# Attention scores from two float32r parts instead of three bf16 parts, the two heads of a pair on the two halves of the TensorE array

## What is computed

```python
q = proj(x1t, Wq, bq); k = proj(x2t, Wk, bk); v = proj(x2t, Wv, bv)
scores = jnp.einsum('bhqd,bhkd->bhqk', q, k) / jnp.sqrt(D_HEAD)   # 512 x 512 a head
attn = jax.nn.softmax(scores, axis=-1)
out = jnp.einsum('bhqk,bhkd->bhqd', attn, v)
...
x = x + jnp.tanh(g_xattn[0]) * xattn(_layernorm(x), ctx_2048, ...)
x = x + jnp.tanh(g_ffn[0]) * ffn(_layernorm(x), ...)               # 8 experts, top 2, one shared
```

## Time and profile before

| | |
|---|---|
| median of 3 runs | 1526.43 us (1523.7 to 1527.67) |
| span of the profiled execution | 1525.5 us; the profile gives no other time of it |
| attention, turns with both kinds of score matmul (i = 0 to 30) | about 47 to 886 us |
| last turn of attention | to about 925 us |
| experts | to the end |

### The profile page before, as it was taken

How to read it: one execution, slowest core, us unless ns; L and a number is a source line. 1 busy time by engine, 2 the same in 40 slices (tenths; PEclk the granted TensorE clock), 3 DMA queues, 4 the chain that set the end, 5 groups by cost and what they waited for, 6 DMA issues and landing times.

```text
span 1525.5 us, 23419 instructions
## 1 busy us (share of the span) xinstructions
PE 1475.7 (97%) x7362; PEld 669.8 (44%) x7362; DVE 887.8 (58%) x1802; ACT 782.5 (51%) x1531; POOL 814.5 (53%) x1241
## 2 busy tenths in 40 slices
PE   5999999999999999999999999989999999999997
PEld 1233333333333333333333328767755454545443
DVE  5888888888888888888888842512221121211111
ACT  2577777777777777777777771100022222222221
POOL 6346675766757667576674443375134444444442
PEclk9999999999999999999999999999999999999999
DMA  6566667766676666765666424785345455554554
GB/s 153 128 160 168 175 167 183 180 161 162 162 177 163 168 163 162 178 170 152 165 154 167 117 92 162 248 213 121 113 76 97 85 96 88 93 91 88 92 90 61
DMA packets 159304, 215.10 MB, mean 141 GB/s; under 512 B 28162, under 2 KB 102416, under 8 KB 158160
## 3 DMA queue, kind: packets, MB, share of 16 engines
q1 hardware_dynamic: 137136, 175.78, 44.9%
q0 software_dynamic: 17952, 37.30, 14.0%
q10 hardware_dynamic: 4096, 0.53, 0.2%
HBM read 126.12 MB, written 86.91 MB: 140 GB/s over the span
## 4 chain that ended last, share of the span: by engine, by line
PE 87%; DMA 6%; DVE 2%; issue 1%; POOL 1%; ACT 1%; SPq 1%; ACTq 0%; POOLq 0%; DVEq 0%
PE bank L1140 16%; PE bank L1062 16%; PE bank L1033 14%; PE bank L1011 14%; PE bank L1160 10%; PE bank L1135 5%; PE bank L996 4%; PE bank L1038 3%; DMA arena<-ht_d 2%; PE bank L1049 2%; PE bank L1000 2%; DMA pv_d<-arena 1%; PE bank L1148 1%; DVE row_max L696 1%; PE bank L1020 1%
## 5 line engine op out<-in xcount | busy, mean ns | idle before, releaser
L696 DVE TENSOR_REDUCE row_max<-bank 128x1 f32<-128x512 f32 x1024 | 664.9, 682 | 111.6 <-PE bank L1011 102.5
L892 ACT ACTIVATE arena<-bank 128x512 f32<-128x512 f32 x1024 | 564.5, 612 | 205.5 <-PE bank L1033 194.0
L1011 PE MATMUL bank<-arena 96*128 96x512 bf16 x1024 | 392.2, 384 | 7.8 <-DVE row_max L696 5.5
L1033 PE MATMUL bank<-arena 98*128 98x512 bf16 x1024 | 387.2, 380 | 2.9 <-ACT arena L892 1.8
L1062 PE MATMUL bank<-arena 128*32 128x512 f32 x2048 | 272.7, 605 | 1.0 <-ACT arena L892 0.7
L1140 PE MATMUL bank<-arena 128*128 x568 | 255.5, 592 | 0.0
L834 DVE TENSOR_TENSOR arena<-arena,bank 128x256 f32<-128x256 f32 x103 | 43.4, 421 | 331.7 <-ACT arena L943 327.9
L943 ACT ACTIVATE arena<-bank 128x256 f32<-128x256 f32 x103 | 39.6, 384 | 378.2 <-PE bank L1140 224.9
L604 POOL DMA_INDIRECT out<-xs,ids x71 | 112.3, 1581 | 226.3 <-ACT xs L954 184.0
L1160 PE MATMUL bank<-arena 128*128 (+1 forms) x412 | 193.8, 593 | 0.9 <-ACT arena L959 0.9
L523 POOL TENSOR_TENSOR arena<-arena 128x512 bf16<-128x512 f32 x62 | 71.6, 1155 | 226.7 <-ACT arena L884 224.0
(11 more groups left out here) (122 smaller groups left out, 1252.4 us busy)
## 6 DMA issues: line engine op xcount, KB each, us to landing
arena<-parts_q SPq DMA_DIRECT2D x64, 256.0 KB, 4.8
pv_d<-arena SPq DMA_DIRECT2D x32, 512.0 KB, 6.3
parts_k<-arena SPq DMA_DIRECT2D x96, 128.0 KB
arena<-parts_k SPq DMA_DIRECT2D x32, 384.0 KB, 4.9
parts_q<-arena SPq DMA_DIRECT2D x96, 128.0 KB
arena<-in_w SPq DMA_DIRECT2D x8, 1536.0 KB, 8.9
h_d<-arena SPq DMA_DIRECT2D x33, 256.0 KB, 6.7
out<-xs SPq DMA_DIRECT2D x33, 256.0 KB, 2.5
```

The lines of the kernel that those rows point to most:

```text
L696: nc.vector.reduce_max(row_max[b % 2][:, u:u + 1], m_ps[(STEPS * b + u) % M_BANKS][:], AX_X).then_inc(s_mx, 1)
L892: nc.scalar.activation(probs[group % 3][:, j, :], e_ps[n % E_BANKS][:], ACT.Exp, scale=float(DH) ** -0.5).then_inc(s_exp, 1)
L1011: nc.tensor.matmul(m_ps[n % M_BANKS][:], q_stack[b % 3][0:STACK, h, qt * P:(qt + 1) * P], k_stack[b % 3][0:STACK, h, :], start=True, stop= ...
L1033: nc.tensor.matmul(e_ps[n % E_BANKS][:], k_stack[b % 3][0:SHIFTED, h, kt * P:(kt + 1) * P], q_stack[b % 3][0:SHIFTED, h, :], start=True, s ...
```

## The change

Keys and queries are now split into two float32r parts, HI and LO. The stacks are `K_PARTS` HI, LO, HI and `Q_PARTS` HI, HI, LO: three times 16 = 48 rows, 50 with the maximum's two. Two heads form a pair: the even head lies on partitions 0 to 49, the odd one on 64 to 113, so a head's matmul reads only rows of one half of the array. In the free dimension there are four pairs instead of eight heads. ACT no longer casts; POOL makes HI (one tensor_scalar) and LO (one subtraction). The order on TensorE changes: both kinds are issued in twos, the two heads of a pair right behind each other, at even steps. For the maxima the order of tiles is now pair, query tile, head, and the column of `row_max` is chosen so that the transposed maxima come out by head. `row` starts four DMAs instead of two.

```diff
-HI, MID, LO = range(3)
-K_PARTS = (HI, MID, LO, HI, MID, HI)
-Q_PARTS = (HI, HI, HI, MID, MID, LO)
+HI, LO = range(2)
+K_PARTS = (HI, LO, HI)
+Q_PARTS = (HI, HI, LO)
...
+PAIR = 2
+READS = PAIR * (len(runs(K_PARTS)) + len(runs(Q_PARTS)))
 STACK = len(K_PARTS) * DH
+SIDE = P // PAIR
 SHIFTED = STACK + 2
...
             def split(b, n):
+                pool.wait_ge(s_evac, 3 * b + n + 1)
+                pool.wait_ge(s_wr[n], 2 * DMA * b)
+                hi, lo = parts[n]
+                nc.gpsimd.tensor_scalar(hi[:], proj[n], 1.0, 0.0, ALU.mult, ALU.add).then_inc(s_hi, 1)
                 pool.wait_ge(s_hi, 2 * b + n + 1)
...
+                nc.gpsimd.tensor_tensor(lo[:], proj[n], hi[:].bitcast(F32), ALU.subtract).then_inc(s_lo, 1)
...
                 act_e.wait_ge(s_mr, 2 * b + half + 1)
-                for n in range(2):
-                    act_e.dma_start(q_stack[b % 3][STACK + n:STACK + n + 1, half * GROUP:(half + 1) * GROUP, :],
-                                    m_rows[half][:, n, :]).then_inc(s_row[half], DMA)
+                for e in range(PAIR):
+                    for n in range(2):
+                        row = e * SIDE + STACK + n
+                        act_e.dma_start(q_stack[b % 3][row:row + 1, 2 * half:2 * half + 2, :].bitcast(F32),
+                                        m_rows[half][e * 2 * KT:(e + 1) * 2 * KT, n, :].bitcast(F32)
+                                        ).then_inc(s_row[half], DMA)
...
             def max_scores(b, u):
-                h, qt = divmod(u, KT)
+                p, qt, e = u // (PAIR * KT), u // PAIR % KT, u % PAIR
+                rows = slice(e * SIDE, e * SIDE + STACK)
...
-                nc.tensor.matmul(m_ps[n % M_BANKS][:], q_stack[b % 3][0:STACK, h, qt * P:(qt + 1) * P],
-                                 k_stack[b % 3][0:STACK, h, :], start=True, stop=True).then_inc(s_ms, 1)
+                nc.tensor.matmul(m_ps[n % M_BANKS][:], q_stack[b % 3][rows, p, qt * P:(qt + 1) * P],
+                                 k_stack[b % 3][rows, p, :], start=True, stop=True).then_inc(s_ms, 1)
...
                 for s in range(STEPS):
-                    if is_b(i):
+                    if s % PAIR == 0 and is_b(i):
                         exp_scores(i, s)
-                    if is_b(i + 1):
+                        exp_scores(i, s + 1)
+                    if s % PAIR == 0 and is_b(i + 1):
                         max_scores(i + 1, s)
+                        max_scores(i + 1, s + 1)
```

More of the change, by code:

```diff
@@ L9 @@
 BF16 = mybir.dt.bfloat16
+F32R = mybir.dt.float32r
 ALU = mybir.AluOpType
@@ L104, in build @@
         xs = sb("xs", [P, B, L])
+        with ExitStack() as stacks:
+            q_stack, k_stack = ([stacks.enter_context(nc.sbuf_tensor(f"{n}_stack{i}", [P, HEADS // PAIR, L], F32R))
+                                 for i in range(3)] for n in "qk")
+            parts = [[stacks.enter_context(nc.sbuf_tensor(f"{n}_{part}", [P, L], F32R)) for part in ("hi", "lo")]
+                     for n in "kq"]
         arena = sb("arena", [P, ARENA])
-        a = Arena(arena)
-        q_stack = [a.take(HEADS * L // 2, BF16).rearrange("p (h l) -> p h l", h=HEADS) for _ in range(3)]
-        k_stack = [a.take(HEADS * L // 2, BF16).rearrange("p (h l) -> p h l", h=HEADS) for _ in range(3)]
+        a = Arena(arena, 6 * HEADS // PAIR * L + 4 * L)
         probs = [a.take(GROUP * L).rearrange("p (j l) -> p j l", j=GROUP) for _ in range(3)]
@@ L113, in build @@
         proj = [a.take(L) for _ in range(2)]
-        rest = a.take(L)
-        parts = [[a.take(L // 2, BF16) for _ in range(3)] for _ in range(2)]
         wq, wk, wv = (a.take(P) for _ in range(3))
@@ L220, in build @@
         s_ones = sem("s_ones")
+        s_stack = sem("s_stack")
         s_x = [sem(f"s_xin{i}") for i in range(4)]
@@ L430, in _ @@
                 if is_b(i + 3):
-                    for part in (HI, MID, LO):
+                    for part in (HI, LO):
                         write(i + 3, 0, part)
@@ L701, in maxima_rows @@
                 if b:
-                    dve.wait_ge(s_row[half], 2 * DMA * b)
+                    dve.wait_ge(s_row[half], 2 * PAIR * DMA * b)
                 return chain(
```

80 lines of the change are left out of this document (29 added, 51 removed).

## The result

| | before | after |
|---|---|---|
| median of 4 runs | 1525.07 us (1520.54 to 1527.67) | 1751.8 us (1730.12 to 1769.05) |
| ratio | | 1.139, interval 1.1327 to 1.1454 |
| span of the profiled execution | 1525.5 us | 1757.5 us |

The ratio compares before with the two faster executions of after (1730.12 and 1744.38 us, mean granted clock 0.925 and 0.903); the other two, 1759.21 and 1769.05 us at 0.890 and 0.885, lie over 1.5% above the fastest, and the first of them is the profiled one. By this ratio the change costs 212 us, by the two medians 227, and not 19: the time is outside the range either way. The four runs lie 39 us apart, against 7 before: the change also made the kernel's time scatter.

A forecast was written before the change was run, and what follows sets the result against it. TensorE bounds the kernel before; after, its loop through three banks: 8 x 2.77 + 4.4, plus 0.6, 0.4 and 0.1, makes 27.7 us a turn against 27.1. Over 31 turns +19 us, start -1.3: 1544 us, range 1505 to 1590.

The forecast's parts named there:

- rival (3): TensorE's granted clock falls for half the time, about +150 us: 1680 us; chance 0.07.
- The chain that takes over: TensorE's loop through three banks of each kind bounds a group of four steps: 2.77 us without the other products.
- E3: Fourth exponentials' product of a four-step group; waits until ACT has read the first one's bank.
- M3: Fourth maxima product of a four-step group; waits for DVE's reduction of the first one's bank, starts at 1.46 us.
- X: TensorE's other products (projections, token transposes, logits, transposed maxima): 4.4 us a turn, added in full after the change.
- p: Weight load that can't be hidden because its instruction waits: 0.09 us more, bounds 0 and 0.19.
- ACT's queue: DMA starts on it hold it 0.56 us each and delay exponentials: 0.4 us a turn, bounds 0 and 2.3.
- The evacuations' 0.6: ACT's copies of K and Q, with the tokens' copy, delay the exponentials behind them: 0.6 us a turn.
- The start: Preparing batch 0's Q parts takes two operations in place of four and ends 1.3 us earlier.
- rival 2: The halves don't overlap or a product takes two passes: turn 29.1 us, 1587 us; chance 0.16.
- rival 4: The loop isn't the bound, TensorE runs ahead and DVE's 23.2 us a turn are: 1405 us; chance 0.04.
- Rival (1): Products run concurrently but waits are shorter, weight loads and DMA starts hidden: 1488 to 1506 us; chance 0.18.

The follow-up runs named there:

- e12: Kernel before, each score product reading 48 of its 96 or 98 rows, order and columns unchanged: 1787.87 us against 1525.62.
- e2: Kernel after plus two overwritten products on half of the rows ahead of the exponentials' products of steps 2, 6, 10 and so on: 1721.99 us, ratio 1.0812.
- e3: Kernel after plus two overwritten 128-row products ahead of the exponentials' products of steps 2, 6, 10 and so on: 1700.93 us, ratio 1.0714.
- e4: Kernel after with two DMA starts in `row` instead of four, each for both halves of the array: 1685.97 us, ratio 1.0591.
- e5: Kernel after with projections, transposed maxima, token transposes and logits moved to other steps, away from the values groups: 1645.02 us, ratio 1.0825.
- e9: Same as e8, but the maxima's rows start at steps 22 and 7 instead of 24 and 9: 1563.48 us, ratio 1.0268.
- e8: Kernel after with two DMA starts in `row` and the values groups moved to the middle of the four steps: 1595.3 us, ratio 1.049.
- e10: Same as e9 plus one 128-row fill product in each of eight places: 1587.11 us, ratio 1.0409; one of four executions took 2131.07.
- e11: Same as e9 plus two 128-row fill products in each of eight places: 1645.01 us, ratio 1.079.

## Why the prediction was wrong

**The step that failed first is the clock.** The sum has no term for it: it took the granted clock as 1.00 in all turns ("PEclk 1.0 in the turns"), and rival (3) had 0.07. The clock was 0.84 on average from 100 to 1100 us, and the fall cost some 108 us; rival (3)'s price of about +150 was of the right order. The argument against it was that streams would fill 63% of a group, "nearer the last turn" than to the place where DVE set the pace. It compared time under streams and never asked how many rows those streams use: e12, with the streams of before on half of the rows, loses at least 229 us. In after two products on half of the rows run side by side, so the rows in use at a time are about as before, but for half of the time, and waits fill the rest; e2 and e3 show that both count, and how much each does isn't known. And the last turn, my example of a safe clock, runs at 0.50 after the change (1110 to 1150 us). I should have seen that no row of before has long stretches of products on half of the rows, so that rows 1 and 9 bear on neither side.

**The second step that failed is the turn at full clock, 27.7 us against 30.2. The chain that takes over: right, 1.4 us a turn too short.** TensorE left being the bound, and E3 and M3 wait for the readers of E0 and M0, as walked. E3 came 1.18 us behind E0, forecast 1.16 (M3's 1.38 less the 0.22 between them). But the group without X is 2.94 us, not 2.77. The term is p: it was charged at M3 alone, but E0 is also a product whose load isn't hidden. Its record lasts 0.50 us where E2's lasts 0.39, M0 starts 0.34 behind it and not 0.22, and ACT starts 0.53 behind it and not 0.42. In all M3 starts 1.53 behind E0 (601.29 to 602.82), forecast 1.46, and the values 0.41 behind M3, whose load isn't hidden either, forecast 0.31. 8 x 0.17 = 1.4 us. That E3 came out almost as forecast is in part luck: the walk had ACT start 0.11 too early and p ahead of E3's start, where it shows in E3's record instead. What the prediction cites for p (the Trainium skill, TensorE: Matmul & The Clock Gate, weight-path perf modes) speaks of FP32 and doesn't name float32r; the records of 0.18 to 0.19 us are what settles it.

**X: a cost that wasn't in the sum.** Each X product stands 0.1 us longer ahead of a score product: a projection 1.06 (592.64 to 593.70) against 0.96, the logits 0.99 against 0.92, the transposed maxima 0.2 against 0.11, and V 1.09 against 0.89. The seven of them make 0.8 us. e12 has it without float32r.

**ACT's queue: too small.** The starts of the DMAs stand 0.66 us apart (four from 594.24 to 596.90), not 0.56, and the extra ones cost 1.2 us a turn (e4), where I took 0.4 for them and 0.1 for late landings. The bound of 2.3 covered it. The chosen value assumed that the group at step 9 gives the delay back; e4 changed both places at once and doesn't tell them apart. The evacuations' 0.6 wasn't isolated; e5 moved all of X, its turns at full clock are 27.8 to 29.9 us, and how much of that is the evacuations' is open. Sum: 27.7 + 1.4 + 0.8 leaves 0.3 for the queue's part beyond what I took, against 30.2 measured; the terms overlap, so e4's 1.2 can't be added on top of all the others.

**The start: wrong sign.** DVE's copy to float32r took 2.03 us at 15.28 (the same copy for K took 0.43 at 7.67; here POOL was clearing `k_stack` from 15.23 on, which may be why), so LO was ready at 18.04, where before the third subtraction ended at 18.47; the first maxima's product came at 29.15 (28.41 before), behind a wait of 3.33 us for the parts of Q read back from DRAM (2.07 before), and the first exponentials' at 55.46 behind a 1.09 us wait for the rows of the maxima (51.26 before): 4.2 us later, not 1.3 earlier.

**What was right.** One pass for a float32r product, two halves side by side (rival 2 is out: one product in 0.39, two in 0.40); DVE isn't the bound (rival 4 is out: busy 23.62 of 30 us in a turn at full clock, 79% where 84% was forecast). Rival (1), shorter waits, is out too, as p is real. Even without the clock's fall the change would have cost some 104 us, still outside the range: what was mis-sized, 2.5 us a turn (30.2 less 27.7), is worth 78 us in 31 turns.

**What stays open.** What exactly makes the clock fall isn't settled. Long waits go with every fall in e9, no wait goes with the falls in e12, and in after the waits are short (0.6 us at most) and come on top of the shorter use of the array. Why seven turns in a row fell in e4 isn't known either. Not tried: e9 without the wait for `pv_d`, long waits with products of full height, and whether the use of rows counts as such or through the numbers that pass.

## What to carry to other kernels

Packing two small products side by side halves their time, and thereby the share of time in which the array is used; if the engine next to it then sets the pace, the clock may fall and take back more than was gained. Ask of each product how many rows it uses, beside how long PE is busy, and read PEclk slice by slice before anything else. At each fall, look for a wait right ahead of it, and when one wait has been taken away, list the waits again: in e9 another had taken its place. Before thinning work on TensorE, see whether it waits for a loop through few buffers: here the place of the values alone was worth up to 3.6 us a turn at full clock (29.02 in e4, 25.4 in e8).

## What the runs showed of the hardware

- With 128-row fills in the eight places of e3, e10 and e11 the granted clock was 1.00 in every full turn of the profiles; one of e10's four executions ran at 0.651 all the same. In e3 that is more work in less time: 1.0714 against 1.139 of the kernel before.
- In e9 each of 13 falls of the clock lies in a turn with a wait of TensorE of 1.5 to 3.7 us, and no turn at full clock has one.
- The same bf16 products on 48 instead of 96 rows, with no gap in PE's records: the clock fell from 1.0 to 0.5 in stretches, 229 to 285 us.
- From a full-height product to one on 48 or 50 rows 0.1 us more; a 128-row fill between a values group and such a product 0.43 us, the second only 0.235.
- A weight load that isn't hidden lengthens the product's record by 0.10 us (0.49 against 0.39) and its reader's start by 0.11.
